# A Mamba block's PSUM banks, small TensorE tiles and a two-state GpSimd product, rearranged inside one large kernel

## The chip, the cores and the metric

One core of a Trainium2 chip runs a whole decoder layer. The metric is the device time of one execution in microseconds. Of three timed executions before the change the median is 1577.21 us (1576.11 to 1578.87). TensorE (PE) multiplies matrices into PSUM, VectorE (DVE) and ScalarE (ACT) read PSUM, GpSimd (POOL) works on SBUF alone, and SyncE (SP) issues DMAs.

## The reference

The input is four sequences of 512 tokens with 256 channels. Three blocks follow each other, each added to its input: two Mamba layers, a cross attention of 16 heads, and a mixture of eight experts beside a shared one. The change lies in the Mamba layers. Cut to what matters, one layer does this for each of the four sequences:

```python
xz = x @ in_w.T; xb, z = split(xz)                 # 512 channels each
xb = silu(causal_conv(xb, 4 taps) + cb)
delta, Bm, Cm = split(xb @ xp_w.T)                 # 16, 16 and 16 columns
delta = softplus(delta @ dtw.T + dtb)
dA = exp(delta[..., None] * -exp(a_log))           # 512 channels x 16 states
mi = delta[..., None] * Bm[:, :, None, :] * xb[..., None]
for t in range(512):
    v = 0.6 * v + mi[t]
    h = dA[t] * h + v
    y[t] = einsum('en,n->e', h, Cm[t])
y = (y + dp * xb) * silu(z);  out = y @ ow.T
```

So there are two recurrences: v with the constant factor 0.6, and h with a factor of its own for each channel, state and token.

## The kernel before

**Groups and states.** A group k is one layer and one sequence: 8 groups. A group has 4 tiles of 128 channels and 16 states, so 64 pieces of work of 128 channels by 512 tokens. Each is called a state here, and steps are numbered r = 0 to 63 in a group. In `pe_mamba`, `dve_mamba`, `act_mamba` and `pool_mamba` the same index i runs over all 512.

**One state.** The recurrence v is a product: the tokens stand in two halves of six chunks (43 or 42 tokens), TensorE multiplies the transposed inputs uT with filters (powers of 0.6 times B; `filt`, built by GpSimd, L925) on 64x64 tiles. One product (L589, 24 matmuls, 48 records in the trace) makes v for two states, and fills two PSUM banks. VectorE scans each state (L748) with the rates `dA` of ScalarE (L889) into a buffer `hst`. GpSimd multiplies the buffer in place by C (L953; C lies in `cb`, loaded by SyncE, one load for eight steps). TensorE transposes the product and adds it to y over the 16 states (`pe_add_state`, L568), LAG = 7 steps after v. Nine buffers hst are kept; two of them are shown as w_early in the trace, since they lie there.

**Side work.** While group k is scanned, the inputs of group k+1 are made, in pieces that the tables `plan_front` and `plan_back` set on a step of each engine: r = 2, 3 normalised input; 8 to 14 the projection p and the output of the group before, bo; 20 xp; 23 to 25 delta; 35 to 38 the gate z; 43 to 48 the transposed u, one chunk a step; 50 the state in the middle of the sequence, mid; 52 to 60 the carry c from each chunk to the next, copied by ScalarE into uT (L854, L855) before the next one can start. TensorE puts a step's piece behind its L568. For the first group this all runs ahead of the states ("the head").

**Banks.** Six PSUM banks are handed out in a ring: `ring()` counts every piece in TensorE's order, the n-th takes bank n mod 6, and `pe_open` waits until the engine that read the bank six pieces ago is through. Where the pair v stands on banks 5 and 0, VectorE scans each state in two parts (L752, L754). Banks 6 and 7 hold y.

**The last group** prepares the attention instead of a next group. SyncE issues 32 small copies (L1013) there, and behind them the load of C for r = 40 on.

## Time and profile before

| what | value |
|---|---|
| median of three executions | 1577.21 us |
| the profiled execution | 1579.04 us, of it the span 1577.5 |
| TensorE busy | 1427.5 us (90%) |
| VectorE, ScalarE, GpSimd busy | 1081.6, 897.0, 923.0 us |
| the multiplications by C (L953), GpSimd | 399 and 113 of them, 517.1 and 145.3 us |
| whole scans (L748), VectorE | 316 and 96, 372.5 and 114.2 us |
| the products v (L589), TensorE | 12288 records, 289.1 us |

The groups of states lie between about 75 and 1005 us; behind them come attention and the experts, which the change does not touch. A busy matmul is one whose end is modelled, so the distance between the starts of two groups of instructions is the better measure of what one costs. TensorE's granted clock in the second to seventh group is 1.00, that is 2.4 GHz. The first state of a group and that of the next are some 115 us apart.

### The profile page before, as it was taken

How to read it: one execution, taken by the hardware profiler on the slowest of the kernel's cores; microseconds unless marked ns; L12 is line 12 of the kernel's file. 1: busy time of each engine (PE TensorE's matmuls, PEld its weight loads, DVE VectorE, ACT ScalarE, POOL GpSimd, SP SyncE). 2: the span in 40 equal slices, each digit the busy share in tenths (PEclk: the TensorE clock that was granted, in tenths of full speed). 3: DMA queues.
4: the chain of work that ended last, by engine and by line, in shares of the span. 5: the costliest groups of instructions: out<-in, count | busy, mean ns of one | idle time of the engine just before them, and what ended most of it. 6: DMA issues, size and time to landing. Idle time of an engine off the chain costs nothing.

```text
span 1577.5 us, 44648 instructions
## 1 busy us (share of the span) xinstructions
PE 1427.5 (90%) x19348; PEld 999.3 (63%) x19348; DVE 1081.6 (69%) x1447; ACT 897.0 (57%) x1287; POOL 923.0 (59%) x802
## 2 busy tenths in 40 slices
PE   4869999999999999999999987878989887999997
PEld 2446676776776776777777775533434343489996
DVE  3298898698698798798797886677666771422223
ACT  2757667667667667667666655216555655434440
POOL 1269878979979979969969976630303000035541
PEclk8889999999999999999999998969999998999999
DMA  4011221222122212212221334470424100612225
GB/s 145 35 52 61 81 82 57 83 82 96 70 83 82 75 63 83 82 66 72 82 83 69 118 134 119 88 147 1 76 45 81 27 1 6 269 41 71 67 68 177
DMA packets 41489, 127.13 MB, mean 81 GB/s; under 512 B 8784, under 2 KB 21584, under 8 KB 32848
## 3 DMA queue, kind: packets, MB, share of 16 engines
q1 hardware_dynamic: 34736, 108.28, 21.3%
q0 software_dynamic: 6048, 14.95, 3.6%
q8 instruction: 155, 2.54, 0.7%
q10 hardware_dynamic: 512, 1.05, 0.4%
q14 instruction: 38, 0.31, 0.1%
HBM read 97.90 MB, written 9.57 MB: 68 GB/s over the span
## 4 chain that ended last, share of the span: by engine, by line
PE 60%; DVE 15%; POOL 9%; issue 9%; ACT 4%; DMA 3%; DVEq 0%; SPq 0%; ACTq 0%; POOLq 0%
PE psum L589 9%; PE psum L568 8%; POOL hst L953 5%; DVE hst L748 4%; PE psum L1264 4%; PE psum L1676 4%; PE psum L1688 3%; PE psum L522 3%; PE psum L559 3%; PE psum L491 3%; PE psum L533 3%; PE psum L1246 2%; PE psum L527 2%; DMA overlay<-x_hat,origin 2%; PE psum L1618 2%
## 5 line engine op out<-in xcount | busy, mean ns | idle before, releaser
L953 POOL TENSOR_TENSOR hst<-hst,cb 128x512 f32<-128x512 f32 x399 | 517.1, 1316 | 137.1 <-DVE hst L748 107.5
L748 DVE TENSOR_TENSOR_SCAN hst<-dA,psum 128x512 f32<-128x512 f32 x316 | 372.5, 1206 | 131.0 <-PE psum L589 130.7
L568 PE MATMUL psum<-ident,hst 128*128 128x128 f32 x1596 | 242.2, 283 | 19.4 <-POOL hst L953 11.4
L568 PEld LDWEIGHTS psum<-ident,hst 128*128 128x128 f32 x1596 | 176.9, 142 | 81.2 <-issue 42.8
L889 ACT ACTIVATE dA<-delta,alog 128x512 f32<-128x512 f32 x256 | 177.7, 719 | 57.2 <-DVE hst L748 29.9
L889 ACT ACTIVATE dA<-xres,alog 128x512 f32<-128x512 f32 x256 | 176.9, 719 | 39.3 <-DVE hst L748 23.2
L1385 DVE TENSOR_REDUCE nmax<-psum 128x2 f32<-128x1024 f32 x128 | 154.6, 1220 | 56.5 <-PE psum L1230 56.2
L1314 ACT ACTIVATE pT<-psum 128x1024 f32<-128x1024 f32 x128 | 128.0, 1024 | 103.1 <-PE psum L1250 79.4
L953 POOL TENSOR_TENSOR w_early<-w_early,cb 128x512 f32<-128x512 f32 x113 | 145.3, 1299 | 26.5 <-DVE w_early L748 22.9
L589 PE MATMUL psum<-filt,c_early 64*64 64x86 f32 (+1 forms) x6144 | 143.9, 238 | 13.3 <-DVE hst L748 5.5
L589 PE MATMUL psum<-filt,uT 64*64 64x86 f32 (+1 forms) x6144 | 145.2, 239 | 9.0 <-DVE w_early L748 2.6
L589 PEld LDWEIGHTS psum<-filt,c_early 64*64 64x64 f32 x6144 | 123.0, 133 | 47.6 <-issue 43.6
L589 PEld LDWEIGHTS psum<-filt,uT 64*64 64x64 f32 x6144 | 123.6, 134 | 41.7 <-issue 38.3
L1921 POOL DMA_INDIRECT overlay<-x_hat,origin x39 | 37.9, 973 | 189.8 <-DVE c_early L1867 178.2
L748 DVE TENSOR_TENSOR_SCAN w_early<-dA,psum 128x512 f32<-128x512 f32 x96 | 114.2, 1205 | 25.8 <-PE psum L589 25.6
L491 PE MATMUL psum<-overlay,w_early 128*128 128x512 f32 x256 | 124.8, 615 | 2.8 <-DVE hst L748 1.1
L1927 POOL DMA_INDIRECT y_choice<-yb,goal x39 | 38.6, 989 | 69.8 <-DVE yb L1881 69.8
L638 DVE SCALAR_TENSOR_TENSOR overlay<-psum,w_cv,overlay 128x509 f32<-128x509 f32 (+2 forms) x96 | 71.2, 744 | 9.3 <-ACT overlay L788 7.1
L1676 PEld LDWEIGHTS psum<-xt,xn 128*128 128x128 f32 x624 | 75.6, 192 | 2.8 <-DVE xt L1873 0.9
L1676 PE MATMUL psum<-xt,xn 128*128 128x128 f32 x624 | 76.1, 275 | 0.7 <-DVE xt L1873 0.7
L1766 ACT ACTIVATE ht<-psum 128x512 f32<-128x512 f32 x39 | 23.3, 597 | 93.6 <-PE psum L1676 93.6
L1688 PE MATMUL psum<-w_down,ht 128*128 x312 | 73.8, 380 | 0.0
(244 smaller groups left out, 2333.7 us busy)
## 6 DMA issues: line engine op xcount, KB each, us to landing
cb<-c_rows SPq DMA_DIRECT2D x64, 1024.0 KB, 4.7
qk_first<-w_early SPq DMA_DIRECT2D x64, 64.0 KB, 2.4
qk<-part SPq DMA_DIRECT2D x64, 64.0 KB, 2.6
w_up<-up_dram SPq DMA_DIRECT2D x8, 512.0 KB, 7.3
w_down<-down_dram SPq DMA_DIRECT2D x8, 512.0 KB, 13.8
w_up<-y_choice SPq DMA_DIRECT2D x8, 512.0 KB, 7.4
qk<-part POOLq DMA_DIRECT2D x48, 64.0 KB, 5.3
qk_first<-part SPq DMA_DIRECT2D x40, 64.0 KB, 2.4
```

Source lines behind the costliest of these rows:

```text
L491: i = pe.matmul(bk, w_in[:, kt, m8 * P:(m8 + 1) * P], xnT[:, kt, :], start=kt == 0, stop=kt == KD - 1)
L568: m = pe.matmul(psum[:, Y0 + et % EP, t * P:(t + 1) * P], hst(i)[:, t * P:(t + 1) * P], ident[:], start=n == 0 and t == 0, stop=n == NSTAT ...
L589: m = pe.matmul(halves_at[half][e0:e0 + MT, :, t0:t0 + width], uT[k % 2][r0:r0 + KT, c, et * P + e0:et * P + e0 + MT], filt[r0:r0 + KT, f ...
L638: i = dve.scalar_tensor_tensor(out=dst, in0=bk[:, 0:S - late], scalar=w_cv[:, l, j, tap:tap + 1], in1=dst, op0=ALU.mult, op1=ALU.add)
L748: dve.tensor_tensor_scan(hst(i), a, v, 0.0, ALU.mult, ALU.add).then_inc(scan_done, 1)
L889: act.activation(dA[:, a % NDA, :], delta[k % 2][:, et, :], ACT.Exp, scale=alog[:, k // B, et, n:n + 1]).then_inc(decay_done, 1)
L953: pool.tensor_tensor(h, h, cb[:, q % 2, state_of(i)[1] % GN, :], ALU.mult).then_inc(g_done, 1)
L1264: m = pe.matmul(psum[i * HROW:(i + 1) * HROW, PV, :], vt[:, cp, kv, c0:c0 + HROW], pT[:, (m0 + i // 2) % NPT, i % 2, :], start=kv == 0, st ...
L1314: act.activation(pT[:, m % NPT], pair(u, "score", s), ACT.Exp, scale=HDIM ** -0.5).then_inc(pair_act, 1)
L1385: dve.tensor_reduce(nmax[:, u % 2, t, 2 * j:2 * j + 2], pair(u, "max", r), AX.X, ALU.max, negate=True).then_inc(pair_dve, 1)
L1676: m = pe.matmul(psum[:, U0 + j % NUB, ft * P:(ft + 1) * P], wu[:, j % NWU, kt * F + ft * P:kt * F + (ft + 1) * P], xt[:, j % NXT, kt, :], ...
L1688: m = pe.matmul(out_bank(j)[:, 0:D], ht[:, j % NHT, ft, :], w_down[:, bass.ds(at + ft * D, D)], start=ft == 0, stop=ft == FT - 1)
```

## The change

What it does, part by part:

- **u** (step 44, 46, 48, two chunks at a time): 96 matmuls of 64x64 with 64 columns instead of 48 of 128x64 with 128. Two banks are filled at once, one by each half of the channels of a tile. ScalarE copies each bank with one instruction, as before.
- **mid**: 12 matmuls on 64x64 tiles with 256 columns instead of 6 of 128x128 with 512; two copies of 256 columns by ScalarE (`act_carry`) instead of one of 512.
- **c**: 4 matmuls on 64x64 tiles with 256 columns, into two banks, instead of one of 128x128 with 512. Four copies of 16x256 instead of two of 16x512.
- **Order on TensorE**: the tiled pieces of a pair of steps stand right behind v; the others stay behind their L568.
- **Banks**: `banks_for` gives each piece the bank that was taken longest ago, and a pair v two neighbours, so the scans in two parts go. In the new hand-out 49 of the pairs v take a bank that the scans of the pair just before leave, instead of 7. Within r = 54 to 60, where the carries are, that is three pairs in an even group and one in an odd one.
- **GpSimd** multiplies two states with one instruction over 1024 columns, and waits for both scans.
- LAG is 6 instead of 7, and eight buffers are kept.
- ScalarE's copy of y waits only for the channel tile of delta whose buffer it overwrites, not for all four.

```diff
@@ after ring() @@
+def banks_for(rows, banks):
+    at, left_by, count, last, oldest = {}, {}, {}, {}, list(range(banks))
+    todo = [(name, who) for name, who in rows]
+    second = None
+    for name, who in todo:
+        count[who] = count.get(who, 0) + 1
+        if second is not None:
+            q, second = second, None
+        elif who == "scan":
+            q = min((b for b in oldest if b + 1 in oldest), key=lambda b: max(oldest.index(b), oldest.index(b + 1)))
+            second = q + 1
+        else:
+            q = oldest[0]
+        oldest.remove(q)
+        oldest.append(q)
+        at[name], left_by[name] = q, last.get(q)
+        last[q] = (who, count[who])
+    return at, left_by
...
-            NDA, AHEAD, LAG, NRING, Y0 = 5, 4, 7, 6, 6
+            NDA, AHEAD, LAG, NRING, Y0 = 5, 4, 6, 6, 6
             NH = LAG + 2
...
+            def hst_pair(i):
+                j = i % NH // 2 * 2
+                return hst_own[:, j:j + 2, :] if j < NH - 2 else spare[:, 0:2, :]
...
                 for c in range(NCH):
-                    put(43 + c, "pe", "u", c)
-                    put(44 + c, "act", "u", c)
+                    put(44 + c // 2 * 2, "pe", "u", c)
+                    put(45 + c // 2 * 2, "act", "u", c)
...
             for i in range(0, NI * TILES, 2):
                 rows += [(("v", i), "scan"), (("v", i + 1), "scan")]
-                for o in (i, i + 1):
-                    rows += [(x, TAKER[x[1]]) for x in steps["pe"].get((o // TILES, o % TILES), [])]
+                for tiled in (True, False):
+                    rows += [(x, TAKER[x[1]]) for x in pair_steps(i) if (x[1] in TILED) == tiled]
...
                 elif what == "u":
-                    bk = pe_open(k, "u", j)
+                    if j % 2:
+                        return
+                    sides = [pe_open(k, "u", j + half) for half in range(2)]
...
-                    for e in range(ET):
-                        for half in range(2):
-                            t0, r0 = half * HS + CHUNKS[j][0], half * KT
-                            i = pe.matmul(bk[r0:r0 + KT, e * P:(e + 1) * P], uw[:, e, t0:t0 + KT], ident[:], start=True, stop=True, tile_position=(0, r0))
+                    for c in range(2):
+                        for e in range(ET):
+                            for half in range(2):
+                                for rows0 in range(0, P, KT):
+                                    t0, c0 = half * HS + CHUNKS[j + c][0], c * HS + e * KT
+                                    i = pe.matmul(sides[rows0 // KT][half * KT:(half + 1) * KT, c0:c0 + KT], uw[rows0:rows0 + KT, e, t0:t0 + KT],
+                                                  ident[rows0:rows0 + KT, rows0:rows0 + KT], start=True, stop=True, tile_position=(rows0, half * KT))
...
                     for c in range(NCH):
-                        i = pe.matmul(bk, bend[:, c, :], uT[par][:, c, :], start=c == 0, stop=c == NCH - 1)
+                        for e0 in range(2):
+                            i = pe.matmul(bk[e0 * MT:(e0 + 1) * MT, e0 * HS:(e0 + 1) * HS], bend[0:KT, c, MID:MID + MT], uT[par][0:KT, c, e0 * HS:(e0 + 1) * HS],
+                                          start=c == 0, stop=c == NCH - 1, tile_position=(0, e0 * MT))
+                elif what == "c":
+                    sides = [pe_open(k, part, j) for part in ("c", "ch")]
+                    pe.wait_ge(bank_act, emptied_by("act", k, "ch", j - 1) if j else emptied_by("act", k, "mid", 0))
+                    for e0 in range(2):
+                        for half in range(2):
+                            r0 = half * KT
+                            i = pe.matmul(sides[half][e0 * MT:(e0 + 1) * MT, e0 * HS:(e0 + 1) * HS], bend[r0:r0 + KT, j, 0:MT],
+                                          uT[par][r0:r0 + KT, j, e0 * HS:(e0 + 1) * HS], start=True, stop=True, tile_position=(r0, e0 * MT))
...
+                        for x in pair_steps(i):
+                            if x[1] in TILED:
+                                pe_side(*x)
                     if i >= LAG:
                         pe_add_state(i - LAG)
                     for x in steps["pe"].get((k, i % TILES), []):
-                        pe_side(*x)
+                        if x[1] not in TILED:
+                            pe_side(*x)
...
-                    b0 = place["v", i - n] % NRING
-                    if b0 < NRING - 1:
-                        v = psum[:, b0:b0 + 2, :].rearrange("p b (t n) -> p n (b t)", n=2)[:, n, :]
-                        dve.tensor_tensor_scan(hst(i), a, v, 0.0, ALU.mult, ALU.add).then_inc(scan_done, 1)
-                    else:
...
+                    b0 = place["v", i - n]
+                    v = psum[:, b0:b0 + 2, :].rearrange("p b (t n) -> p n (b t)", n=2)[:, n, :]
+                    dve.tensor_tensor_scan(hst(i), a, v, 0.0, ALU.mult, ALU.add).then_inc(scan_done, 1)
...
+            def act_carry(dst, bk):
+                for e0 in range(2):
+                    cols = slice(e0 * HS, (e0 + 1) * HS)
+                    i = act.copy(dst[0:NSTATE, cols], bk[e0 * MT:e0 * MT + NSTATE, cols])
+                i.then_inc(bank_act, 1)
...
                     act.wait_ge(y_full, ET * k + j + 1)
-                    act.wait_ge(delta_done, ET * min(k + 2, NI))
+                    act.wait_ge(delta_done, ET * (k + 1) + j + 1 if k + 1 < NI else ET * NI)
...
                 elif what in ("c", "ch"):
...
+                    act.wait_ge(bank_full, filled(k, "ch", j))
+                    act_carry(uT[par][KT * (what == "ch"):, j + 1, :], bank(k, what, j))
...
-                    h = hst(i)
-                    pool.wait_ge(scan_done, i + 1)
-                    pool.tensor_tensor(h, h, cb[:, q % 2, state_of(i)[1] % GN, :], ALU.mult).then_inc(g_done, 1)
+                    if i % 2 == 0:
+                        h, n = hst_pair(i), state_of(i)[1] % GN
+                        pool.wait_ge(scan_done, i + 2)
+                        pool.tensor_tensor(h, h, cb[:, q % 2, n:n + 2, :], ALU.mult).then_inc(g_done, 2)
```

On TensorE, in group 2 (counted from 0), steps 44 to 47 (here L589, L568 and L522 are v, adding to y, and u). Before:

```order
L589 MATMUL psum<-filt,c_early 64x2x43 x16
L589 MATMUL psum<-filt,c_early 64x2x42 x8
L568 MATMUL psum<-ident,hst 128x128 x4
L522 MATMUL psum<-ident,overlay 64x128 x8
L568 MATMUL psum<-ident,hst 128x128 x4
L522 MATMUL psum<-ident,overlay 64x128 x8
L589 MATMUL psum<-filt,c_early 64x2x43 x16
L589 MATMUL psum<-filt,c_early 64x2x42 x8
L568 MATMUL psum<-ident,hst 128x128 x4
L522 MATMUL psum<-ident,overlay 64x128 x8
L568 MATMUL psum<-ident,hst 128x128 x4
L522 MATMUL psum<-ident,overlay 64x128 x8
```

and in the changed program, where the same three are L634, L613 and L553:

```order
L634 MATMUL psum<-filt,c_early 64x2x43 x16
L634 MATMUL psum<-filt,c_early 64x2x42 x8
L553 MATMUL psum<-ident,overlay 64x64 x32
L613 MATMUL psum<-ident,w_early 128x128 x8
L634 MATMUL psum<-filt,c_early 64x2x43 x16
L634 MATMUL psum<-filt,c_early 64x2x42 x8
L553 MATMUL psum<-ident,overlay 64x64 x32
L613 MATMUL psum<-ident,hst 128x128 x8
```

Four groups of u, two behind each pair v, have become two, each right behind v; the L568 of both steps now stand together.

On TensorE in the same group, steps 50 to 54 (L533 is mid, L527 a carry). Before:

```order
L589 MATMUL psum<-filt,c_early 64x2x43 x16
L589 MATMUL psum<-filt,c_early 64x2x42 x8
L568 MATMUL psum<-ident,hst 128x128 x4
L533 MATMUL psum<-uT,overlay 128x512 x6
L568 MATMUL psum<-ident,hst 128x128 x4
L589 MATMUL psum<-filt,c_early 64x2x43 x16
L589 MATMUL psum<-filt,c_early 64x2x42 x8
L568 MATMUL psum<-ident,hst 128x128 x4
L527 MATMUL psum<-uT,overlay 128x512
L568 MATMUL psum<-ident,hst 128x128 x4
L589 MATMUL psum<-filt,c_early 64x2x43 x16
L589 MATMUL psum<-filt,c_early 64x2x42 x8
```

and in the changed program (L564 and L572):

```order
L634 MATMUL psum<-filt,c_early 64x2x43 x16
L634 MATMUL psum<-filt,c_early 64x2x42 x8
L564 MATMUL psum<-uT,overlay 64x256 x12
L613 MATMUL psum<-ident,hst 128x128 x8
L634 MATMUL psum<-filt,c_early 64x2x43 x16
L634 MATMUL psum<-filt,c_early 64x2x42 x8
L572 MATMUL psum<-uT,overlay 64x256 x4
L613 MATMUL psum<-ident,w_early 128x128 x8
L634 MATMUL psum<-filt,c_early 64x2x43 x16
```

The middle state and the carry now stand ahead of both transposes of their pair, in the same tile shape as v.

On GpSimd, steps 34 to 41 of the first group (L910 is u, L915 the gate). Before:

```order
L925 TENSOR_TENSOR filt<-toep,bcol 128x516
L953 TENSOR_TENSOR w_early<-w_early,cb 128x512 x2
L953 TENSOR_TENSOR hst<-hst,cb 128x512
L910 TENSOR_TENSOR overlay<-delta,xbs 128x512
L953 TENSOR_TENSOR hst<-hst,cb 128x512
L910 TENSOR_TENSOR overlay<-delta,xbs 128x512
L925 TENSOR_TENSOR filt<-toep,bcol 128x516
L953 TENSOR_TENSOR hst<-hst,cb 128x512
L910 TENSOR_TENSOR overlay<-delta,xbs 128x512
L953 TENSOR_TENSOR hst<-hst,cb 128x512
L910 TENSOR_TENSOR overlay<-delta,xbs 128x512
```

and in the changed program (L991, L962, L947 and L952 in the place of L953, L925, L910 and L915):

```order
L962 TENSOR_TENSOR filt<-toep,bcol 128x516
L991 TENSOR_TENSOR hst<-hst,cb 128x1024 x2
L947 TENSOR_TENSOR overlay<-delta,xbs 128x512 x2
L962 TENSOR_TENSOR filt<-toep,bcol 128x516
L991 TENSOR_TENSOR w_early<-w_early,cb 128x1024
L947 TENSOR_TENSOR overlay<-delta,xbs 128x512
L952 TENSOR_TENSOR xres<-xres,overlay 128x512
L947 TENSOR_TENSOR overlay<-delta,xbs 128x512
L991 TENSOR_TENSOR hst<-hst,cb 128x1024
```

Two u follow one multiplication of two states where one u followed each.

## Rows read from the trace of the kernel before

**Rows 1.** Busy us (instructions) of PE, PEld, DVE, ACT, POOL, then clock, DMA share, GB/s

```profile
430.00:545.00 115.00, 111.22 (x2045) 82.90 (x2034) 96.23 (x113) 78.32 (x124) 98.93 (x80) 1.00 0.20 76
485.00:508.00 23.00, 20.59 (x361) 14.42 (x360) 19.84 (x22) 17.13 (x26) 22.93 (x18) 1.00 0.13 48
```

**Rows 2.** Chain of waits: start us, us, work; first and last of six middle states

```profile
291.96 5.15 PE psum L533 x12
...
869.12 5.15 PE psum L533 x12
```

**Rows 3.** What TensorE waited for in 430 to 545 (us, times, longest)

```profile
PE psum L522 <- POOL overlay L910: 1.1, 1, 1.1
PE psum L568 <- ACT xraw L805: 1.0, 1, 1.0
PE psum L589 <- ACT xres L792: 0.5, 1, 0.5
```

**Rows 4.** Timeline of TensorE: start us, us, instructions; a pair of states alone

```profile
465.38 1.12 PE L589 MATMUL psum<-filt,uT 64*64 64x86 f32 x48
466.43 1.09 PE L568 MATMUL psum<-ident,hst 128*128 128x128 f32 x8
467.45 1.12 PE L589 MATMUL psum<-filt,uT 64*64 64x86 f32 x48
```

**Rows 5.** The same view: u, the middle state, one carry

```profile
511.07 1.09 PE L522 MATMUL psum<-ident,overlay 128*64 128x128 f32 x16
512.09 0.66 PE L568 MATMUL psum<-ident,hst 128*128 128x128 f32 x4
...
522.76 5.32 PE L533 MATMUL psum<-c_early,overlay 128*128 128x512 f32 x12
527.92 0.60 PE L568 MATMUL psum<-ident,hst 128*128 128x128 f32 x4
...
529.99 1.02 PE L527 MATMUL psum<-c_early,overlay 128*128 128x512 f32 x2
530.85 0.60 PE L568 MATMUL psum<-ident,hst 128*128 128x128 f32 x4
```

**Rows 6.** The same view: a product on 128x64 tiles

```profile
469.08 1.95 PE L498 MATMUL psum<-overlay 128*64 128x256 f32 x16
```

**Rows 7.** Timeline of ScalarE: first copy of a carry, and what follows its second

```profile
531.05 0.58 ACT L854 COPY c_early<-psum 16x512 f32<-16x512 f32 x1 [1.00 <-PE psum L527]
...
532.24 1.34 ACT L889 ACTIVATE dA<-delta,alog 128x512 f32<-128x512 f32 x2
```

**Rows 8.** Timeline of VectorE: two split scans start, and two whole ones

```profile
433.37 0.66 DVE L752 TENSOR_TENSOR_SCAN hst<-dA,psum 128x256 f32<-128x256 f32 x1
...
434.73 0.66 DVE L752 TENSOR_TENSOR_SCAN hst<-dA,psum 128x256 f32<-128x256 f32 x1
...
448.09 2.32 DVE L748 TENSOR_TENSOR_SCAN hst<-dA,psum 128x512 f32<-128x512 f32 x2
```

**Rows 9.** Timeline of GpSimd: multiplications by C between two filters

```profile
515.22 3.73 POOL L953 TENSOR_TENSOR hst<-hst,cb 128x512 f32<-128x512 f32 x3
518.91 1.06 POOL L925 TENSOR_TENSOR filt<-toep,bcol 128x516 f32<-128x516 f32 x1
```

**Rows 10.** Costliest groups, GpSimd: one multiplication over 1024 columns

```profile
L1490 POOL TENSOR_TENSOR xres<-xres,b_o 128x1024 f32<-128x1024 f32 x4 | 9.5, 2366 | 0.0
```

**Rows 11.** Timeline of TensorE in the head: carries

```profile
68.25 1.43 PE L527 MATMUL psum<-c_early,overlay 128*128 128x256 f32 x4 [0.48 <-ACT c_early L855]
69.84 1.43 PE L527 MATMUL psum<-c_early,overlay 128*128 128x256 f32 x4 [0.16 <-ACT c_early L855]
```

**Rows 12.** Timeline of ScalarE in the head: one copy of 256 columns

```profile
68.13 0.36 ACT L854 COPY c_early<-psum 16x256 f32<-16x256 f32 x1
```

**Rows 13.** Timelines of the last group: SyncE's issues, GpSimd behind them

```profile
941.50 24.30 SPq L1013 DMA_DIRECT2D qk_first<-w_early  x32
...
971.04 1.26 POOL L953 TENSOR_TENSOR hst<-hst,cb 128x512 f32<-128x512 f32 x1 [13.97 <-DMA cb<-c_rows]
```

83 lines of the change are left out of this document (36 added, 47 removed).

## The prediction

> **What bounds the kernel now.** I read the page first, for the span (in the table), then the busy times by stretch, then the chain of waits, then TensorE's waits and the timelines of one group of states. The table shows TensorE busiest. The chain goes through the middle state of every group; the first and the last of six stand at 291.96 and 869.12 us [rows 2], so a group takes 577.16 / 5 = 115.4 us. In one of them (115 us), TensorE is busy for 111.2, GpSimd 98.9, VectorE 96.2, ScalarE 78.3 [rows 1]. So TensorE is the bound over a group, with about 3.8 us of gaps, and what it no longer has to do should come back, until GpSimd or a wait stands in its place. The reader should also see the second row there: from 485 to 508 GpSimd is full (22.9 of 23.0 us) and TensorE is not (20.6). The bound moves inside a group. Of TensorE's waits 1.1 us are for GpSimd's u, 1.0 for ScalarE's copy of y and 0.5 for its copy of z [rows 3]; the last two come of one thing, a copy of y that waits for four pieces of delta.
>
> A pair of states alone costs TensorE 467.45 - 465.38 = 2.07 us [rows 4]. GpSimd needs (518.91 - 515.22) / 3 = 1.23 for a state [rows 9], so 2.46 a pair, and 1.06 more for a filter every second pair in the second half of a group.
>
> **The change, part by part, for one group that makes inputs for a next one (seven of eight).**
>
> u. Before, one chunk of 16 records costs 512.09 - 511.07 = 1.02 us, six of them 6.1 [rows 5]. Now there are 192 records, on four small tiles, 64 columns each. The nearest row is v, the same tiles and 86 columns, 48 records in 466.43 - 465.38, 1.05 us (the start of what follows) [rows 4], so 0.022 a record. 192 x 0.022 = 4.2 us. If the cost falls with the columns it is 3.1; if the tiles overlap no better than today's two (0.064 a record for twice the columns) it is 6.1. I take 4.2: gain 1.9, from 0 to 3.
>
> mid. Before, 527.92 - 522.76 = 5.16 us [rows 5]. Now 24 records of 256 columns, two tiles side by side. The nearest row has 16 records of 256 columns on two tiles in 1.95 us, 0.12 each [rows 6]. 24 x 0.12 = 2.9. Gain 2.3; nothing, if the two tiles ran one after the other (24 x 0.21, half of 5.16 / 12).
>
> Carries. On TensorE one costs 530.85 - 529.99 = 0.86 us [rows 5], in a pair of 2.07 + 0.86 = 2.93. On four tiles it would be 8 records, 0.5 us (four at once) to 1.0 (0.12 each), so the pair could be 2.5 to 3.0. But ScalarE now makes four copies. Before, two copies take 532.24 - 531.05 = 1.19 us and the two rates behind them 1.34 [rows 7], 2.5 in all. A copy of 256 columns is 0.36 us in the head [rows 12], so four take 1.5 and ScalarE needs 1.5 + 1.3 = 2.8 us a pair. The next carry waits for the last copy. GpSimd needs 2.4 + 0.5 = 2.9 there. So the pair costs 2.8 to 2.9 instead of 2.93, and TensorE's gain of 5 x 0.4 turns into a wait for ScalarE: I count nothing (from -1 to +2).
>
> The page TensorEngine Tiling (Array Packing) of the Trainium skill, section PSUM Bottleneck, says that tiles speed up TensorE but not the emptying of PSUM, which may become the bottleneck. The trace agrees as far as it goes: the copy of half the columns costs 0.36 and not 0.29 us.
>
> Waits that go. GpSimd's u: TensorE comes to it after v(44) instead of after step 42's pieces, at least 1.05 us later, and GpSimd is a little earlier; the 1.1 us go. The copy of y waits for its own tile of delta: 1.0 + 0.5 go. Together 2.6, from 1 to 2.6. What is late next is GpSimd (below).
>
> Split scans. Two split ones start 434.73 - 433.37 = 1.36 us apart, two whole ones take 2.32 together, 1.16 each [rows 8]. On 100 of the 512 states that is 20 us of VectorE, 2.5 a group. VectorE is not the bound, so I count 0.7 (0 to 1).
>
> Banks. 49 pairs v instead of 7 wait for the scans just before them, six or seven more a group. Where side work of 3 us or more stands between, it costs nothing. In the carries there are only 0.5 + 1.0 us of TensorE between v and v, while two scans take 2.3 + 0.1, so TensorE stands for 0.9 (1.0 at most) and VectorE then for one product, and the pair takes 2.4 + 1.1 = 3.5 instead of 2.8. That is three pairs in an even group and one in an odd one: 1.4 on average, of which 0.7 is left against 2.93 because nothing was counted for the others. At step 40 it is 0.4 more. Cost 1.1, from 0 to 3.
>
> GpSimd. The only instruction over 1024 columns is 2.37 us [rows 10], with another operand; two of 512 columns are 2.46. I take 2.36, so 0.1 a pair and 1.6 in half a group, with 2.46 and 2.26 as the ends. This puts nothing into the sum by itself, it keeps GpSimd off the path: 32 x 2.46, 8 filters at 1.06 and 8 u and gates at 1.23 are 97.0, so 1.9 of its 98.9 us are spent in slower instructions beside VectorE. Its second half of a group costs 16 x 2.46 + 8.5 + 6 x 1.23 + 1.9 = 57 us, and becomes 55. TensorE gains some 5.5 in the same half, so GpSimd falls 4 us further behind than before. The eight buffers let it lag by two or three pairs, some 6 us, and it catches up in r = 8 to 16, where TensorE has eight pieces of side work and GpSimd none. It just fits. The shorter LAG and the wait for both scans cost a pair's multiplication of slack (2.4 us), and I see no place before where that slack was used: TensorE never waited long for L953 outside the last group.
>
> Sum for a group: 1.9 + 2.3 + 0 + 2.6 + 0.7 - 1.1 = 6.4 us, and 7 x 6.4 = 45.
>
> The last group has no u, mid or carry. GpSimd sits 13.97 us until C is there, at 971.04, behind 32 issues that take 24.30 us from 941.50 [rows 13]. That start follows work of step 28, so only the 12 pairs behind it gain, 12 x 0.1 = 1.2 us, less 0.5 since both last states come at once: +0.7. In the head, u gains 1.9 and mid 2.3, but a carry step of 69.84 - 68.25 = 1.59 [rows 11] becomes 0.5 for the product, 4 x 0.37 for the copies and twice 0.16, the wait shown there, for the hand-overs: 2.3, five times 0.7 = 3.5. With one copy more behind u and mid it comes to nothing (from -3 to +2).
>
> 45 + 1 = 46 us. The profiled execution took 1579.0, the median is 1577.2, 1.8 lower; 1579.0 - 46 = 1533, and against the median 1531.
>
> **The rivals.**
>
> GpSimd becomes the bound. For it: full from 485 to 508 already, and it has 2.4 us of slack less. Against it: 115 - 98.9 = 16 us idle in a group. If its instruction costs 2.46 for two and the lag is used up, TensorE gives the 1.6 us of a half back in waits: 6.4 - 1.6 = 4.8 a group, 34 in all, 1543.
>
> The carries gain after all. If ScalarE gets its rates done while TensorE works, a pair is 2.5 or 2.6, and if the filled banks don't bind either, a group gains 2 + 1.1 more: 9.5 x 7 = 66, 1511.
>
> The tiles don't pay. If small tiles run mid and u at the price of today (no gain in the two terms), 4.2 a group go: 2.2 x 7 + 1 = 16, 1561. Against it: the rows of v and of the 128x64 tiles.
>
> Slower, by the banks. Each of the 42 added waits stops TensorE and then VectorE, since neither has work ahead. At 0.9 + 1.1 us each they cost 84 us; the other terms bring 7 x 7.5 + 1 = 54. Then it is 1577 + 30 = 1607. It decides from 54 / 42 = 1.3 us a wait on. For it: no bank is left over where three pieces share six banks. Against it: 28 of them stand where TensorE has side work of 3 us and more between the two v.
>
> **How the numbers follow.** The sum: 0.46. GpSimd's bound: 0.17. The carries' gain: 0.16. No gain from tiles: 0.10. Slower by the banks: 0.08. No change (0.2%, 3 us, about what a measurement of this kernel can tell from none): 0.03. The first four are all faster, 0.89; same 0.03; slower 0.08. The ends of the terms give 2.5 to 10 us a group, so 1559 to 1508; the range is 1508 to 1562, which holds the first three and the fourth just so.
>
> **What would show it.** In the changed profile the middle states should be 109 us apart. u should take 1.4 us for 64 records, mid 2.9, a carry 0.5 to 1.0. TensorE should wait for ScalarE's copies in r = 54 to 60, and there, in even groups, for scans. L991 should be about 2.4 us, and no scan in two parts left. Wrong would be: long waits of TensorE for L991 (GpSimd's bound, or too few buffers), pairs of 3.5 us outside the carries (the banks), u or mid at their old price.

## The result, and the profile after

The changed kernel takes 1585.31 us (median of 5 runs, 1583.6 to 1588.39), the one before 1577.21 (1575.34 to 1578.87): a ratio of 1.0054, 95% interval 1.0039 to 1.0069. It is slower by 8 us, where 1531 was forecast, with a range of 1508 to 1562. The profiled execution has a span of 1582.1 us.

The page after, busy times and the shares of the chain of waits. The table of before had TensorE at 1427.5 us and VectorE at 1081.6.

```profile
PE 1375.0 (87%) x20442; PEld 982.1 (62%) x20442; DVE 1097.7 (69%) x1347; ACT 908.0 (57%) x1365; POOL 876.3 (55%) x546
...
PE 52%; DVE 24%; issue 11%; POOL 5%; ACT 4%; DMA 3%; SPq 1%; DVEq 0%; POOLq 0%; ACTq 0%
```

TensorE has 52 us less to do. VectorE, which lost its 100 split scans and a third of one product's columns, has 16 us more, and its share of the chain rises from 15% to 24%. That is what to look at first.

TensorE's timeline after: two middle states, then u, middle state and a carry (beside [rows 2], [rows 5]).

```profile
296.33 2.76 PE L564 MATMUL psum<-c_early,overlay 64*64 64x256 f32 x24
...
522.70 1.10 PE L553 MATMUL psum<-ident,overlay 64*64 64x64 f32 x64
523.73 1.09 PE L613 MATMUL psum<-ident,hst 128*128 128x128 f32 x8
...
528.85 2.76 PE L564 MATMUL psum<-c_early,overlay 64*64 64x256 f32 x24
531.54 1.09 PE L613 MATMUL psum<-ident,hst 128*128 128x128 f32 x8
...
533.50 0.61 PE L572 MATMUL psum<-c_early,overlay 64*64 64x256 f32 x8
534.04 1.09 PE L613 MATMUL psum<-ident,w_early 128*128 128x128 f32 x8
...
876.41 2.76 PE L564 MATMUL psum<-uT,overlay 64*64 64x256 f32 x24
```

u costs 1.03 us for 64 records instead of 2.04 for 32, the middle state 2.69 instead of 5.16, a carry 0.54 instead of 0.86. But the groups are (876.41 - 296.33) / 5 = 116.0 us apart, against 115.4. Where inside a group the time is, in us, mean of the five groups from 291.8 (296.3 after) on, each stretch from the start of its first TensorE instruction to the next's:

| stretch | before | after | single products (below) |
|---|---|---|---|
| middle state to last carry (r = 50 to 60) | 19.0 | 17.1 | 17.1 |
| to xp (r = 60 to 64, 0 to 20) | 42.9 | 44.6 | 44.5 |
| xp to first d (r = 20 to 23) | 5.5 | 5.5 | 5.5 |
| first d to last z (r = 23 to 38) | 23.6 | 27.6 | 23.8 |
| last z to u (r = 38 to 44) | 10.1 | 11.0 | 10.7 |
| u to middle state (r = 44 to 50) | 14.4 | 10.2 | 10.3 |
| sum | 115.4 | 116.0 | 112.0 |

The last column is the kernel a_single, the change with one GpSimd instruction for each state. Its profiled execution, at 1557.96 us, was the longest of its four (1544.96 to 1557.96, median 1550.3), so the column shows less than the medians do.

The tiles' gain is there, 1.9 and 4.1 us. It is given back between, most of it from the first d to the last z. The two profiled executions, before and after, are 4.6 us apart: 4.5 of it arise before the first of these middle states, 2.9 in the five groups, and 2.9 come back behind the last. Busy times of that stretch, in the same group of before, after and a_single (columns as in [rows 1]: length, then PE, PEld, DVE, ACT, POOL):

```profile
474.59:498.25 23.66, 23.40 (x466) 16.75 (x465) 22.70 (x29) 18.79 (x28) 20.95 (x16) 1.00 0.24 91
```

```profile
479.53:506.12 26.59, 24.19 (x469) 17.16 (x469) 26.56 (x25) 21.59 (x34) 18.33 (x9) 1.00 0.20 82
```

```profile
470.18:493.95 23.77, 23.77 (x470) 17.16 (x469) 22.68 (x25) 21.19 (x33) 21.54 (x17) 1.00 0.26 92
```

Before, TensorE is full and VectorE nearly so (22.70 of 23.66). After, VectorE has fewer instructions (25 against 29) and is busy in 26.56 of 26.59 us, and TensorE is not full. GpSimd is less busy than before. So VectorE's instructions became longer. After, its timeline and GpSimd's in this stretch:

```profile
484.97 0.39 DVE L700 TENSOR_SCALAR xraw<-xres 128x512 f32<-128x512 f32 x1
485.29 1.21 DVE L786 TENSOR_TENSOR_SCAN hst<-dA,psum 128x512 f32<-128x512 f32 x1
486.42 1.46 DVE L700 TENSOR_SCALAR xraw<-xres 128x512 f32<-128x512 f32 x1
487.80 1.21 DVE L786 TENSOR_TENSOR_SCAN hst<-dA,psum 128x512 f32<-128x512 f32 x1
...
500.58 1.21 DVE L786 TENSOR_TENSOR_SCAN hst<-dA,psum 128x512 f32<-128x512 f32 x1
501.71 2.73 DVE L710 TENSOR_TENSOR xres<-xres,xraw 128x512 f32<-128x512 f32 x1
504.37 1.21 DVE L786 TENSOR_TENSOR_SCAN hst<-dA,psum 128x512 f32<-128x512 f32 x1
505.50 0.66 DVE L710 TENSOR_TENSOR xres<-xres,xraw 128x512 f32<-128x512 f32 x1
```

```profile
485.22 2.38 POOL L991 TENSOR_TENSOR hst<-hst,cb 128x1024 f32<-128x1024 f32 x1 [2.62 <-DVE hst L786]
...
501.55 2.35 POOL L991 TENSOR_TENSOR hst<-hst,cb 128x1024 f32<-128x1024 f32 x1
505.72 2.65 POOL L991 TENSOR_TENSOR hst<-hst,cb 128x1024 f32<-128x1024 f32 x1 [1.82 <-DVE hst L786]
```

The clip L700 takes 0.39 us when GpSimd is idle as it starts, and 1.46 when it starts inside L991: it ends at 487.88, and L991 at 487.60. The maximum L710 starts at 501.71, just behind L991, and ends at 504.44; L991 ends at 503.90. The scans, which read PSUM, take 1.21 either way. GpSimd then waits for the scan behind the held-off maximum (1.82 us at 505.72), and TensorE for GpSimd. The duration in the profile holds the wait: no view shows it as a wait. Three groups of VectorE's, the maximum L710, the product of the coefficients L694 and the clip L700, after, and then before (L666, L650, L656):

```profile
L710 DVE TENSOR_TENSOR delta<-delta,xraw 128x512 f32<-128x512 f32 x16 | 22.1, 1379 | 0.0
L694 DVE TENSOR_TENSOR overlay<-bcol,ends 128x192 f32<-128x192 f32 x8 | 15.8, 1970 | 0.3
L700 DVE TENSOR_SCALAR xraw<-delta 128x512 f32<-128x512 f32 x16 | 14.3, 894 | 0.0
```

```profile
L666 DVE TENSOR_TENSOR delta<-delta,xraw 128x512 f32<-128x512 f32 x16 | 13.8, 863 | 0.0
L650 DVE TENSOR_TENSOR overlay<-bcol,ends 128x288 f32<-128x288 f32 x8 | 10.3, 1291 | 0.3
L656 DVE TENSOR_SCALAR xraw<-delta 128x512 f32<-128x512 f32 x16 | 7.3, 455 | 0.0
```

With the other halves of L710 and L700 (21.2 and 12.9; before 13.1 and 7.1) they went from 51.6 to 86.3 us.

TensorE's waits after, from 200 to 880 us (total, times, longest), and behind the dots two of before:

```profile
PE psum L553 <- POOL overlay L947: 11.6, 6, 2.2
PE psum L634 <- DVE hst L786: 11.4, 11, 1.9
PE psum L634 <- DVE w_early L786: 10.1, 8, 1.8
PE psum L613 <- POOL hst L991: 10.0, 10, 1.3
PE psum L604 <- DVE hst L786: 6.8, 4, 2.3
...
PE psum L568 <- ACT xraw L805: 6.7, 6, 1.3
PE psum L522 <- POOL overlay L910: 6.3, 6, 1.1
```

The waits for ScalarE's copies are gone, and the wait for GpSimd's u has grown from 6.3 to 11.6 us. The waits for scans (L786) and for L991 are new at this size.

### The profile page after: what moved, and what is told of

The parts are those of the page before. It is cut to its first block, busy times and chain, and to the rows that moved or that the text cites. A ratio compares the mean times of both kernels' runs of the same rounds, so it can differ in the third digit from the quotient of the medians.

```text
span 1582.1 us, 46724 instructions
## 1 busy us (share of the span) xinstructions
PE 1375.0 (87%) x20442; PEld 982.1 (62%) x20442; DVE 1097.7 (69%) x1347; ACT 908.0 (57%) x1365; POOL 876.3 (55%) x546
## 3 DMA queue, kind: packets, MB, share of 16 engines
q10 hardware_dynamic: 512, 1.05, 0.4%
## 4 chain that ended last, share of the span: by engine, by line
PE 52%; DVE 24%; issue 11%; POOL 5%; ACT 4%; DMA 3%; SPq 1%; DVEq 0%; POOLq 0%; ACTq 0%
DVE hst L786 10%; PE psum L634 8%; PE psum L613 6%; PE psum L1302 4%; PE psum L1714 4%; PE psum L1726 4%; PE psum L604 3%; DVE w_early L786 3%; PE psum L1284 2%; PE psum L518 2%; POOL overlay L947 2%; PE psum L1656 2%; PE psum L553 2%; PE psum L1268 2%; DVE nmax L1423 2%
## 5 line engine op out<-in xcount | busy, mean ns | idle before, releaser
L991 POOL TENSOR_TENSOR hst<-hst,cb 128x1024 f32<-128x1024 f32 x192 | 455.0, 2379 | 175.0 <-DVE hst L786 165.0
L786 DVE TENSOR_TENSOR_SCAN hst<-dA,psum 128x512 f32<-128x512 f32 x384 | 447.6, 1203 | 110.6 <-PE psum L634 110.5
L613 PE MATMUL psum<-ident,hst 128*128 128x128 f32 x1536 | 222.1, 282 | 29.0 <-POOL hst L991 25.9
L613 PEld LDWEIGHTS psum<-ident,hst 128*128 128x128 f32 x1536 | 168.8, 142 | 72.4 <-POOL hst L991 30.1
L1352 ACT ACTIVATE pT<-psum 128x1024 f32<-128x1024 f32 x128 | 128.0, 1024 | 104.6 <-PE psum L1288 103.4
L786 DVE TENSOR_TENSOR_SCAN w_early<-dA,psum 128x512 f32<-128x512 f32 x128 | 150.8, 1205 | 47.4 <-PE psum L634 47.2
L991 POOL TENSOR_TENSOR w_early<-w_early,cb 128x1024 f32<-128x1024 f32 x64 | 151.7, 2371 | 41.9 <-DVE w_early L786 41.9
L634 PE MATMUL psum<-filt,c_early 64*64 64x86 f32 (+1 forms) x6144 | 150.3, 243 | 27.2 <-DVE hst L786 16.8
L634 PEld LDWEIGHTS psum<-filt,c_early 64*64 64x64 f32 x6144 | 128.8, 138 | 64.0 <-issue 40.2
L634 PE MATMUL psum<-filt,uT 64*64 64x86 f32 (+1 forms) x6144 | 144.6, 238 | 16.6 <-DVE w_early L786 7.8
L634 PEld LDWEIGHTS psum<-filt,uT 64*64 64x64 f32 x6144 | 123.2, 133 | 49.7 <-issue 41.7
L613 PE MATMUL psum<-ident,w_early 128*128 128x128 f32 x512 | 77.7, 290 | 1.8 <-POOL w_early L991 1.8
## 6 DMA issues: line engine op xcount, KB each, us to landing
w_down<-down_dram SPq DMA_DIRECT2D x8, 512.0 KB, 12.9
```

Source lines behind the costliest of these rows:

```text
L613: m = pe.matmul(psum[:, Y0 + et % EP, t * P:(t + 1) * P], hst(i)[:, t * P:(t + 1) * P], ident[:], start=n == 0 and t == 0, stop=n == NSTAT ...
L634: m = pe.matmul(halves_at[half][e0:e0 + MT, :, t0:t0 + width], uT[k % 2][r0:r0 + KT, c, et * P + e0:et * P + e0 + MT], filt[r0:r0 + KT, f ...
L786: dve.tensor_tensor_scan(hst(i), a, v, 0.0, ALU.mult, ALU.add).then_inc(scan_done, 1)
L991: pool.tensor_tensor(h, h, cb[:, q % 2, n:n + 2, :], ALU.mult).then_inc(g_done, 2)
L1352: act.activation(pT[:, m % NPT], pair(u, "score", s), ACT.Exp, scale=HDIM ** -0.5).then_inc(pair_act, 1)
```

## The experiments

Before took 1575.6 to 1577.5 us (medians) beside them. Ratios are to before, with the 95% interval.

### The GpSimd instruction

a_two_short: both states in two instructions, behind the wait for both scans.

```
-pool.tensor_tensor(h, h, cb[:, q % 2, n:n + 2, :], ALU.mult).then_inc(g_done, 2)
+for o in (i, i + 1):
+    pool.tensor_tensor(hst(o), hst(o), cb[... of o ...], ALU.mult).then_inc(g_done, 1)
```

> The changed kernel, but GpSimd multiplies the two states in two instructions of 512 columns, both still behind the wait for both scans. Theory 1, the long GpSimd instruction holds off VectorE's instructions that read and write SBUF alone (delta's maximum L710, its clip L700, bend L694, 34.7 us longer in all): these fall back to 0.4 and 0.7 us in the median, and about 35 us go, 1550 us. Theory 2, the hand-out of banks costs the gain: they may get shorter but the time stays within 5 us of 1585. Theory 3, the wait for both scans: also no change here, maybe 5 us slower by 256 x 0.1 us of GpSimd.

a_single: each state alone and behind its own scan, the rest as after.

```
-pool.wait_ge(scan_done, i + 2)      # every second i
+pool.wait_ge(scan_done, i + 1)      # every i, one instruction each
```

> The changed kernel, but GpSimd multiplies each state by itself and waits for its own scan alone; LAG stays 6, with eight buffers. Theory 1: the same as the two short instructions, 1550 us, within 4. Theory 3, the wait for both scans costs on its own: 10 us or more below the two short instructions. Theory 2: still near 1585.

Measured: 1575.73 (1.000, 0.998 to 1.002) and 1550.3 (0.9824, 0.9791 to 0.9857). a_two_short lies between its theories (1550, or within 5 of 1585). a_single is at the 1550 of theory 1, but not level with a_two_short: it is 25 us below, as theory 3 had it (10 or more). Of the 35 us, 10 go with the length of the instruction and 25 more when GpSimd may start behind each scan. VectorE's three kinds, 86.3 us after, took 61.1 and 52.6: three quarters of their extra time went with the length, but only 10 of the 35 us did. So the time that VectorE is held off is not the whole cost. In a_two_short the stretch from the first d to the last z takes 25.2 us (27.6 after, 23.8 in a_single), and 1.7 us a group more than in a_single lie in the other stretches; its waits for GpSimd's u are 16.3 us from 200 to 880 (12.3 in a_single). With single products the change is 26 us faster than before.

b_y_lag6 and b_y_pair put the same into the kernel before. LAG 6 comes with the copy of y that waits for its own tile; it wasn't tried without it.

```
-NDA, AHEAD, LAG, NRING, Y0 = 5, 4, 7, 6, 6
+NDA, AHEAD, LAG, NRING, Y0 = 5, 4, 6, 6, 6
-act.wait_ge(delta_done, ET * min(k + 2, NI))
+act.wait_ge(delta_done, ET * (k + 1) + j + 1 if k + 1 < NI else ET * NI)
```

> The kernel before with two edits: LAG 6 (eight buffers) and the copy of y that waits for its own tile of delta. Theory 1: no loss from the LAG, and 1.5 us a group from the copy of y: 1577 - 10 = 1567 us. Theory 3, the shorter LAG costs: 1577 or more.

> The same, and GpSimd multiplies two states in one instruction, nothing else of the change. Theory 1: about 35 us more than the one before it less what TensorE's gaps hide, so 1590 us, with the clip, the maximum and bend as long as in the changed kernel. Theory 2: within 3 us of the one before it, since the banks are as before.

Measured: 1592.91 (1.0095, 1.006 to 1.013) and 1644.86 (1.0436, 1.0398 to 1.0475). The instruction over two states, with its wait for both scans, costs 52 us there, more than the 35 of theory 1. That b_y_lag6 was itself slower than before, by 16, only its theory 3 allowed, without a size; it is taken up below.

Where in a group does it cost? a_pair_half and a_pair_out use it only for some r.

```
+if i % TILES < TILES // 2:                        # a_pair_half
+if i % TILES < 22 or i % TILES >= 46:             # a_pair_out
     (two states in one instruction)
+else:
+    (one state, behind its own scan)
```

> The kernel after with the instruction over two states in the first half of each group alone (r below 32) and single ones in the second, where u and the gates stand. Theory 1 (the pair instruction costs where GpSimd is full and VectorE has delta to make; in the first half GpSimd has slack): 1550 to 1560, near the 1550.3 of single ones everywhere. Rival (each of the pairs costs alike): half of the 35 us stay, 1563 to 1572.

> The kernel after with single multiplications only for r = 22 to 45 of each group, where VectorE makes the coefficients of the middle state, clips and maximises the four tiles of delta (nine instructions whose operands lie all in SBUF), and the instruction over two states everywhere else. Pairs in the first half alone measured 1582.8. Theory 1 (what the long instruction costs is VectorE held off in just this stretch, where it has no idle time left: 27.5 of 27.5 us busy): nearly all comes back, 1550 to 1558, and the stretch from the first d to the last z takes about 24 us as with single ones, not 27.5. Rival (each pair that TensorE and GpSimd wait for costs, wherever it stands): 24 of 64 states are single, so a third to a half of the 35 us comes back, 1568 to 1575.

Measured: 1582.75 (1.0036, 1.0024 to 1.0048) and 1553.01 (0.9859, 0.9821 to 0.9897). The first missed both expectations: my reason for it, that GpSimd is full only in the second half, was wrong, since pairs below r = 32 alone keep nearly the whole cost (1582.75 of 1585.31). The second hit. With 40 of 64 states still in pairs nearly all of the 35 us are back: it matters only what GpSimd does at r = 22 to 45, where VectorE has nine instructions with all operands in SBUF. These meet short instructions here (the three kinds take 52.4 us in all), and GpSimd doesn't wait for a second scan there either; this run does not part the two. The stretch from the first d to the last z, in a_pair_half and in a_pair_out:

```profile
482.85:509.07 26.22, 23.97 (x469) 17.18 (x469) 26.19 (x25) 21.23 (x34) 19.78 (x11) 1.00 0.24 83
```

```profile
468.75:492.51 23.76, 23.76 (x469) 17.14 (x469) 22.68 (x25) 21.18 (x33) 21.51 (x17) 1.00 0.23 92
```

m_port measures by itself, in one execution, whether VectorE's instructions are held off.

> A small kernel of its own that computes nothing of the reference (its output is a copy of x): seventeen stages, in each eight VectorE instructions of one kind over 128x512 (maximum of two SBUF operands, minimum with a constant, scan with the second operand in PSUM, maximum with the second in PSUM, scan with both in SBUF), alone, beside eight GpSimd multiplications of 512 columns, and beside four of 1024. Theory (VectorE's instructions whose operands all lie in SBUF can't start while a GpSimd instruction runs; those with a PSUM operand can): the maximum of two SBUF operands takes about 0.55 us alone, 1.2 to 1.8 on average beside the short ones and 1.8 to 3 beside the long ones; the minimum likewise from 0.3; the scan and the maximum from PSUM stay within 10% of their time alone. Rival (the instructions share bandwidth, nothing is held off): every kind is slower by the same factor beside short and long ones, 1.1 to 1.5, and none reaches the length of GpSimd's instruction.

VectorE's instructions in m_port (ns: least, median, most). The maximum alone, beside 512 columns on GpSimd, beside 1024; then the minimum, likewise; then scan and maximum with an operand in PSUM, and the scan with both operands in SBUF, all 24 of each in one row:

```profile
L45 DVE TENSOR_TENSOR to<-a,b x8: 682/682/692, 13.8 to 18.0; 128x512 f32<-128x512 f32 x8
L45 DVE TENSOR_TENSOR to<-a,b x8: 1744/1744/1779, 18.8 to 30.5; 128x512 f32<-128x512 f32 x8
L45 DVE TENSOR_TENSOR to<-a,b x8: 677/1750/2860, 32.3 to 45.2; 128x512 f32<-128x512 f32 x8
...
L48 DVE TENSOR_SCALAR to<-a x8: 419/420/427, 45.9 to 48.3; 128x512 f32<-128x512 f32 x8
L48 DVE TENSOR_SCALAR to<-a x8: 1478/1478/1516, 48.8 to 58.7; 128x512 f32<-128x512 f32 x8
L48 DVE TENSOR_SCALAR to<-a x8: 412/1485/2595, 60.2 to 71.2; 128x512 f32<-128x512 f32 x8
...
L51 DVE TENSOR_TENSOR_SCAN to<-a,psum x24: 1193/1194/1220, 71.7 to 98.4; 128x512 f32<-128x512 f32 x24
L54 DVE TENSOR_TENSOR to<-a,psum x24: 678/679/689, 100.0 to 119.0; 128x512 f32<-128x512 f32 x24
L57 DVE TENSOR_TENSOR_SCAN to<-a,b x24: 1192/1719/3394, 124.2 to 167.1; 128x512 f32<-128x512 f32 x24
```

The kinds that read SBUF alone take up to 2.86 and 2.60 us beside the long instruction, those that read PSUM never change. A scan with both operands in SBUF went from 1.20 to 3.39 at most, so it is the operands, not the operation. It goes both ways: GpSimd's own instruction over 512 columns takes 1.26 us alone, and 1.70 (median) beside the maxima. The rival of shared bandwidth is out: the factor is 1.0 or up to 6, by kind. This is what the Trainium skill says, SBUF — State Buffer, section "Who interferes with whom": a VectorE instruction in a two-port mode or with two inputs in SBUF and a GpSimd instruction take turns at a shared port pair, and the second blocks in full until the first ends. The rows agree.

### LAG 6, and the copy of y

b_y is before with the second line of the diff above alone.

> The kernel before with only the wait of the copy of y changed (its own tile of delta instead of all four). With LAG 6 as well it measured 1592.9. Theory 1 (LAG 6 is what costs; the copy's wait gives 1 to 2 us a group): 1563 to 1575. Rival (the copy that comes earlier upsets ScalarE's order and costs the 16 us itself): 1588 to 1595.

Measured: 1586.35 (1.0063, 1.0044 to 1.0082), just under the rival's range: 10 us slower by a wait that was taken away. TensorE around the first u, in b_y:

```profile
511.99 1.09 PE L568 MATMUL psum<-ident,hst 128*128 128x128 f32 x8
515.91 1.62 PE L522 MATMUL psum<-ident,overlay 128*64 128x128 f32 x16 [2.83 <-POOL overlay L910]
517.46 1.99 PE L589 MATMUL psum<-filt,uT 64*64 64x86 f32 x48
```

Its busy times and granted clock (the column behind POOL) before u, at u and behind it:

```profile
512.90:515.90 3.00, 0.18 (x2) 0.02 (x1) 2.66 (x3) 1.26 (x2) 3.00 (x4) 1.00 0.23 35
...
517.46:519.40 1.94, 1.94 (x51) 1.76 (x49) 0.00 (x0) 1.21 (x2) 1.94 (x2) 0.50 0.67 275
520.10:524.30 4.20, 4.20 (x89) 3.49 (x88) 2.11 (x3) 2.42 (x4) 4.20 (x5) 1.00 0.01 4
```

From the middle state to u it takes 101.1 us with and without the edit: u waits for GpSimd, whose row of products, u and filters has no gap there. The 1.5 us that the copy of y no longer holds up are added to the wait for u (17.7 us from 200 to 880, against 6.3). Before, TensorE's idle time came in pieces of 1.0, 0.5 and 1.1 [rows 3]; here it is one of 3 us, and behind it the granted clock stands at 0.50 (1.2 GHz) and v takes 1.92 us instead of 1.05. From 200 to 900 us the busy time times what the granted clock lacks of 1.00 (in windows of 4 us) adds up to 0.0 in before, 7.2 in b_y, 11.5 in b_y_lag6. It fits group by group: from u to the middle state b_y takes 2.7, 1.5, 1.4, 0.0 and 1.3 us more than before, and the clock lacks 2.7, 1.7, 1.4, 0.0 and 1.3 there. The changed kernel has this loss too, 7.1 us.

LAG 6 adds 6.5 more. GpSimd's timeline in b_y_lag6:

```profile
512.77 1.28 POOL L910 TENSOR_TENSOR overlay<-xres,overlay 128x512 f32<-128x512 f32 x1
513.99 1.28 POOL L953 TENSOR_TENSOR w_early<-w_early,cb 128x512 f32<-128x512 f32 x1
515.22 1.28 POOL L915 TENSOR_TENSOR sz<-sz,xbs 128x512 f32<-128x512 f32 x1
516.43 1.11 POOL L910 TENSOR_TENSOR overlay<-xres,overlay 128x512 f32<-128x512 f32 x1
```

LAG is part of the sum for the step of the gate L915. With 7 it is step 40 and stands behind the last u (L910), with 6 it is 39 and stands in front. The runs with the suffix ug put it back, in before and in after:

```
-steps["pool"].setdefault((k, s + 3), []).append((k, "gate", e))
+steps["pool"].setdefault((k, s + 4 - e), []).append((k, "gate", e))
```

> The kernel before with LAG 6 and the copy of y that waits for its own tile (1592.9 measured), and GpSimd's first gate of a group one step later, r = 40 instead of 39. LAG sets the step of that gate, and with 6 it came to stand ahead of the last u on GpSimd. Theory 1 (this one instruction ahead of u is all that LAG 6 costs against LAG 7): back to the 1586.4 of LAG 7 with the same copy, 1583 to 1589; TensorE's wait for u from 200 to 880 us falls from 24.9 to about 17.7 us. Rival (LAG 6 costs by its eight buffers): stays at 1590 to 1595.

> The kernel after with the gate behind the last u, nothing else. Theory 1: 5 to 10 us faster than after's 1585.3, 1575 to 1580. Rival (with the instruction over two states VectorE's chain delta, u sets the time and not GpSimd's order): 1582 to 1587.

> The kernel after with single multiplications by C (1550.3 measured) and the gate behind the last u on GpSimd as well. Theory 1: TensorE's wait for u (12.3 us in six groups, the longest 2.4) falls by 1.2 a group and its clock no longer falls there: 1538 to 1546. Rival (GpSimd has as much to do as before, so what u gains the next product loses): 1548 to 1552.

Measured: 1580.87 (1.0024, 1.0014 to 1.0034), 12 us less than without and below the 1583 to 1589 of theory 1 (5 less than b_y with LAG 7, which no run explains); 1579.19 (1.0008, 0.9992 to 1.0023), 6 less than after, as theory 1 had it; 1555.92 (0.9857, 0.9834 to 0.9881), where 1550.3 was (above both ranges; the intervals overlap: no gain). TensorE's wait for u in the first fell from 24.9 to 17.5 us. So the gate's place is worth 6 us in the changed kernel as it is, and the loss by the clock fell with it, from 7.1 to 1.7 us. With single products the wait for GpSimd's u fell from 12.3 to 5.7 us, but 4.5 us in front of u now have no releaser in the profile; the loss by the clock fell from 8.4 to 2.6, and the time did not follow. So there something else sets the time.

a_single_ring7_oldy is the tiles and the order of after with single products, LAG 7, banks in turn (a_single_ring7, below) and the old wait of the copy of y.

> Single multiplications, LAG 7, banks in turn (1565.0 measured, with the tiles and the order of after), and the copy of y that waits for all four tiles of delta as before. Theory 1 (the old wait spreads TensorE's idle time, so that its clock doesn't fall at u; in the kernel before it was worth 10 us): 1555 to 1561. Rival (the forecast's: the copy of y costs 1.5 us a group): 1572 to 1577.

Measured: 1561.13 (0.9909, 0.9882 to 0.9936), 4 below a_single_ring7, with overlapping intervals. There the old wait costs nothing, and may bring a little.

### Banks and buffers

a_single_7 is a_single with LAG 7 and nine buffers, a_single_ring7 that with the banks in turn and the split scans of before.

```
-place, left_by = banks_for(rows, NRING)
+turn_of, taken = ring(rows)
+place = {x: n % NRING for x, n in turn_of.items()}
+left_by = {x: taken[n - NRING] if n >= NRING else None for x, n in turn_of.items()}
```

> The kernel after with each state multiplied by C by an instruction of its own, behind its own scan, and with LAG 7 and nine state buffers as before (so two parts of the change are undone together). It measured 1550.3 with single instructions and LAG 6. Theory 1 (the instruction over two states is what costs, and the ninth buffer gives GpSimd and TensorE more room): 1530 to 1543, and TensorE's wait for GpSimd's u (L553), 12.3 us from 200 to 880 us at LAG 6, falls to 6 or less. Rival (the buffer count is worth nothing once the instruction is short): 1547 to 1553, L553's wait still near 12.

> The same, and the PSUM banks handed out in turn as before, with the scans of a pair in two parts where its banks wrap around. What is left of the change is the four-tile u, middle state and carries, u in front of the added states, and the copy of y that waits for its own tile. Theory 1 (the banks by idle time cost a little more in waits for the scans just before than they save in split scans): 2 to 6 us faster than the run a_single_7 of this same chip. Rival (split scans cost VectorE more than the waits cost TensorE): 3 to 10 us slower than it. My forecast's terms (1.9 u, 2.3 mid, 2.6 waits a group, 7 groups) would give 1577 - 48 = 1529 here.

Measured: 1559.66 (0.9898, 0.9865 to 0.993) and 1565.03 (0.9926, 0.9902 to 0.9951). The first missed both its ranges: LAG 7 with its ninth buffer makes it slower, not faster. In a_single_7 the product L601 (the output of the group before) waits 11.4 us in all, up to 4.7. The profile names no releaser; the program has it wait for GpSimd's last gate, which comes one state later with LAG 7. That this is the whole difference was not tried. Banks by idle time are 5 us better than banks in turn by the medians, as the rival had it (3 to 10), where theory 1 had them 2 to 6 worse; the two intervals overlap, so that they are better is not shown.

a_single_bank gives pairs only banks from an even one on, and side pieces one of the oldest three away from a scan's. By the program's order 7 pairs wait for the scans just before them, where it was over 40.

```
-q = min((b for b in oldest if b + 1 in oldest), key=...)
+q = min((b for b in oldest if b % 2 == 0), key=...)
-q = oldest[0]
+q = min(oldest[:3], key=lambda b: ("scan" in (last.get(b, " ")[0], last.get(b ^ 1, " ")[0]), oldest.index(b)))
```

> The kernel after with single multiplications (1550.3 measured) and another rule for the PSUM banks: a pair of inputs takes only two banks that begin at an even number, and a side piece takes, of the three oldest banks, one whose neighbour and which itself were not left by a scan, if there is one. By the order of the program 7 pairs of inputs then wait for the scans just before them instead of 49 (or 42 without the head), and no scan is in two parts. Theory 1 (the waits for filled banks, 13.5 us of TensorE from 200 to 880 us and the 1.1 us a group by which the carries are slower than with banks in turn, are real): 1538 to 1546. Rival (the next thing, GpSimd's u or ScalarE's copies, ends at the same time): 1548 to 1552.

> The same with the gate behind the last u on GpSimd. Theory 1 (once the banks no longer hold TensorE, it comes earlier to u and waits longer there, and the gate's 1.2 us count): 3 to 8 us faster than a_single_bank. Rival (as with banks by idle time, where it moved 1550.3 to 1555.9, no gain): within 3 us or slower.

Measured: 1549.23 (0.9822, 0.9787 to 0.9857) and 1551.7 (0.985, 0.982 to 0.988), both as their rivals had it. The carries are faster, 15.7 us instead of 17.1, and all of it is lost again by xp, 46.2 instead of 44.5. The chain of waits of a_single_bank:

```profile
PE 48%; POOL 25%; DVE 11%; issue 10%; ACT 4%; DMA 2%; DVEq 0%; SPq 0%; ACTq 0%; POOLq 0%
```

GpSimd has 25% of it, against 9% in before and 17% in a_single. Its busy time in a group of 112 us is 98.8, what it was in 115 before. The last two runs ask whether it is the bound. They leave out 480 of the 512 columns of each gate.

```
-pool.tensor_tensor(sz[par][:, j, :], sz[par][:, j, :], xbs[par][:, j, NSTATE:NSTATE + S], ...)
+pool.tensor_tensor(sz[par][:, j, 0:32], sz[par][:, j, 0:32], xbs[par][:, j, NSTATE:NSTATE + 32], ...)
```

> The kernel with single multiplications and the other bank rule (1549.2 measured), with GpSimd's four gates of a group (the product of silu(z) and y) over 32 of 512 columns; the other 480 columns are left out, so its output is not the reference's. That takes some 4 us of GpSimd's 98.8 in a group of 112. Theory 1 (GpSimd is the bound once VectorE is not held off and the banks are free): 20 to 30 us faster, 1520 to 1530. Rival (TensorE is still the bound, 105.6 of 112 busy): 1543 to 1550.

> The kernel before with the gates over 32 of 512 columns in the same way (480 columns left out, the output not the reference's). Theory 1 (there TensorE is the bound and GpSimd's row of u ends just with it): 0 to 10 us faster than before, 1567 to 1577, most of it in the wait for u. Rival (GpSimd was as much the bound before): 20 to 30 us faster.

Measured: 1526.54 (0.9663, 0.9622 to 0.9705), 22.7 us less for some 4 us of GpSimd in each of eight groups; and 1569.31 (0.9959, 0.994 to 0.9978), 7 less, both as their theories 1 had it. VectorE's three kinds take the same in a_bank_gate32 and a_single_bank (52.6 and 52.5 us), so the gain does not come by them. TensorE's waits without a releaser in front of L604, the output of the group before, fell from 11.1 to 1.1 us, which bears out that this product waits for the gates. The loss by the clock fell too, from 4.0 to 0.0 us, and may be part of the 22.7. So GpSimd's work bounds the kernel with single products and free banks, and far less the one before.

The fastest whole kernels are a_single (1550.3) and a_single_bank (1549.23), equal by their intervals, 26 us faster than before and 35 faster than the change.

## Why the prediction was wrong

In one line, from these runs: 1576 before, +10 by the copy of y (1586), +7 by LAG 6 with the gate ahead of u (1593), -43 by tiles, order and banks (1550), +35 by the GpSimd instruction over two states (1585). The forecast had the third too small (27 us) and the other three at nothing or with the wrong sign. The terms hold in this order only: with single products the old wait of the copy of y and the place of the gate move nothing beyond the intervals.

**"This puts nothing into the sum by itself", and "I see no place before where that slack was used".** This is the step that failed: +35 us in place of about 0. The instruction's own length was right (2.38 us by L991, 2.36 taken). Wrong was to ask only what it costs GpSimd. VectorE's clip, maximum and coefficient product of r = 23 to 38 are held off while it runs; their durations grew by 35 us in all (that this is also the kernel's loss is chance, since a_two_short took 25 of them back and gained 10), on an engine busy 22.70 of 23.66 us there, though the forecast called VectorE "not the bound" from its mean over a group (96.2 of 115). The larger part hangs on what the forecast called slack that isn't used: with both scans waited for, GpSimd starts late, and that is 25 us of the 35 by a_two_short against a_single. That the place is r = 22 to 45 is shown by a_pair_out. How the 25 us come about, by the later start itself or by the order in which the two engines then meet, stays open. A row of before pointed to it, the maximum's least, median and most in ns for one shape:

```profile
L666 DVE TENSOR_TENSOR xres<-xres,xraw x16: 658/681/1511, 47.0 to 729.7; 128x512 f32<-128x512 f32 x16
```

**Waits that go, 2.6 us a group.** The 1.5 us for ScalarE's copies went, and came back in the wait for GpSimd's u, which the forecast had at nothing and which grew (11.6 us from 200 to 880, against 6.3). Taking the copy's wait away made before 10 us slower. The forecast read three waits and did not ask what they all run into: GpSimd's u, at the same time with or without them. And it had no term for the clock, which fell behind the longer wait. That the clock is the cause is read from the rows, group by group; no run holds the clock up by itself.

**"GpSimd is a little earlier."** It is later, since LAG 6 puts a gate in front of the last u. a_ug shows 6 us for it.

**u 1.9, mid 2.3.** Right in kind, too small: the work fell by 3.0 and 2.5 us, the stretch from u to the middle state by 4.1 with the lower clock behind the wait for u, and by 5.3 without it (9.07 us from u at 751.98 to the middle state at 761.05, at a granted clock of 1.00).

**Carries 0.** Between: TensorE's part fell by 0.3 each, and the ten steps from the middle state on take 1.9 us less, 3.3 less without the filled banks. Neither ScalarE's four copies nor the rival's full gain.

**Split scans +0.7, banks -1.1.** Together -0.4 us a group was forecast, and with single products the medians say +5 us in all (a_single_7 against a_single_ring7), which the intervals do not separate from nothing. The waits for filled banks are there, 1.4 us in the carries, but another engine ends at the same time, and a_single_bank gains 1 us in all, which is within the intervals.

**The head, nothing.** That came out: the first v starts at 75.43 us, against 75.26. From 60 to 80 us TensorE is busy 9.3 us instead of 15.1, at a mean granted clock of 0.57 instead of 1.00.

**The rivals.** "GpSimd becomes the bound" had 0.17 and 1543. Its sign, waits of TensorE for L991, is there (10.0 us in ten pieces), but GpSimd is idle in front of L991 in that stretch, waiting for scans. It is what holds the kernel once the long instruction is gone: a_bank_gate32 against b_gate32. Slower than before (0.08) was given to the banks, at r = 54 to 60 and others; it came at r = 22 to 45, where VectorE is held off and GpSimd starts late, by a mechanism that was not among the rivals.
